# A graph network in f32: group sums in four PSUM banks, a pair's finishing a round later, and the counting as a loop

## The reference, cut to what matters

```
deg  = max(count of src, 1);  cnt = count of dst
msg  = (t1[src] + (x[src] * x[dst]) @ W2) / sqrt(deg[src] * deg[dst])      t1 = x @ W1
e    = leaky_relu(where(cnt > 0, t1 + segment_sum(msg, dst), 0) + b)
x1   = layernorm(x + e / max(norm(e), 1e-12))
agg  = segment_sum((x1 @ W.T + b1)[src], dst) / (count of dst + 1)
out  = layernorm(x1 + agg)
```

## Time and profile before

| | us |
|---|---|
| median of 3 runs (3993.7 to 3995.43) | 3994.8 |
| the profiled execution | 3996.79 |
| its span, first to last instruction | 3995.1 |

### The profile page before, as it was taken

The page is one execution under the profiler, slowest core; times in us unless marked ns, Lnnn a source line. Parts: engine busy times, 40 slices in busy tenths (PEclk is TensorE's granted clock), DMA queues, the critical chain, the costliest instruction groups (busy, mean ns, idle before and its releaser), DMA issues.

```text
span 3995.1 us, 42771 instructions
## 1 busy us (share of the span) xinstructions
PE 2991.8 (75%) x10186; PEld 1828.7 (46%) x10186; DVE 1864.8 (47%) x3536; ACT 664.3 (17%) x2054; POOL 2982.0 (75%) x3146
## 2 busy tenths in 40 slices
PE   4551777777777777777777877888888888878887
PEld 4441555555555555555433333344334343334443
DVE  9994555555555555555423333333333323232323
ACT  7992111111111111111100000000000000000000
POOL 7776777777777777777667777777777777777776
PEclk5555888988888888888867777666766666776667
DMA  8878455555555555555334443434443434343433
GB/s 256 272 233 309 150 156 155 155 156 155 156 155 155 156 158 156 158 155 156 116 94 118 117 118 116 119 115 120 115 120 115 120 115 120 115 121 114 120 115 107
DMA packets 294217, 582.43 MB, mean 146 GB/s; under 512 B 60723, under 2 KB 176100, under 8 KB 294180
## 3 DMA queue, kind: packets, MB, share of 16 engines
q0 software_dynamic: 150048, 409.93, 35.4%
q1 hardware_dynamic: 131364, 159.19, 11.9%
q10 hardware_dynamic: 12768, 12.85, 0.9%
HBM read 506.27 MB, written 75.45 MB: 146 GB/s over the span
## 4 chain that ended last, share of the span: by engine, by line
POOL 65%; issue 23%; POOLq 1%; PE 1%; DVE 0%; DVEq 0%; DMA 0%; ACT 0%; SPq 0%; ACTq 0%
POOL ring L478 65%; PE banks L1095 0%; POOLq L511 0%; DVEq L688 0%; POOLq L475 0%; PE banks L1121 0%; POOLq L476 0%; PE banks L1084 0%; DMA ring<-scaled_x,idx 0%; DMA ring<-x,idx 0%; POOL ring L488 0%; DMA x<-out_t 0%; DVE stats L917 0%; DVE out_t L929 0%; DVE big L850 0%
## 5 line engine op out<-in xcount | busy, mean ns | idle before, releaser
L1121 PE MATMUL banks<-ring,hot_space 128*128 128x257 f32 x6252 | 2470.7, 521 | 806.8 <-DMA ring<-x,idx 330.9
L1121 PEld LDWEIGHTS banks<-ring,hot_space 128*128 128x128 f32 x6252 | 1309.8, 242 | 1896.2 <-DMA ring<-x,idx 1058.0
L478 POOL DMA_INDIRECT ring<-x,idx x1563 | 1486.9, 951 | 505.3 <-issue 475.9
L478 POOL DMA_INDIRECT ring<-scaled_x,idx x1281 | 1221.2, 953 | 402.7 <-issue 402.7
L850 DVE SCALAR_TENSOR_TENSOR big<-banks,here_mask,big 128x257 f32 x784 | 343.9, 480 | 1604.5 <-PE banks L1121 1604.3
L806 DVE TENSOR_TENSOR hot_space<-banks,dst_rel 128x1024 f32<-128x1024 f32 x395 | 483.5, 1225 | 212.6 <-issue 210.8
L592 ACT COPY idx<-src_col 128x8 int32 (+1 forms) x392 | 77.3, 197 | 2145.7 <-PE banks L1121 2145.7
L488 POOL DMA_INDIRECT ring<-in_x,src_col x276 | 264.1, 957 | 84.1 <-issue 84.1
L554 ACT ACTIVATE dst_rel<-columns,halves 128x128 bf16<-128x128 f32 (+1 forms) x896 | 253.5, 374 | 23.8 <-PE banks L1042 19.6
L1035 PE MATMUL banks<-hot_space 128*128 128x98 bf16 x1120 | 104.2, 283 | 139.2 <-DVE hot_space L695 139.2
L1095 PE MATMUL banks<-w_s,a_t 128*128 128x256 f32 x784 | 179.3, 383 | 0.0
(11 more groups left out here) (115 smaller groups left out, 1193.2 us busy)
## 6 DMA issues: line engine op xcount, KB each, us to landing
kept_rows<-ring SPq DMA_DIRECT2D x94, 384.0 KB, 3.4
ring<-kept_rows SPq DMA_DIRECT2D x47, 768.0 KB, 5.5
ring<-x,idx POOLq DMA_INDIRECT x1563, 2.8
ring<-scaled_x,idx POOLq DMA_INDIRECT x1281, 2.8
dst_col<-in_src SPq DMA_DIRECT2D x47, 384.0 KB, 5.8
scaled_x<-big ACTq DMA_DIRECT2D x14, 896.0 KB, 17.5
x<-out_t SPq DMA_DIRECT2D x98, 128.0 KB, 2.4
x_t<-x SPq DMA_DIRECT2D x98, 128.0 KB, 2.3
```

The costliest lines, as they stand in the source:

```text
L478: g.indirect_dma_start(ring[:, u, 0:D], None, table[layer], bass.IndirectOffsetOnAxis(ap=idx[:, u:u + 1], axis=0)).then_inc(rows_in[u], 16)
L1121: last = nc.tensor.matmul(group_sum(k % SUMS), dst_hot[:, k % HOTS, u - k * GT, :], ring[:, u, 0:DW], start=u == tiles[0], stop=u == tiles ...
```

## The change

- `SUMS` is 4: group sums use banks 0 to 3, and VectorE's look-up of the kept factors (`found`) moves from banks 2 and 3 to banks 4 and 5, which the transposes use as well; TensorE therefore waits for `r_kept_made` before the transposes.
- A pair's transposes stand behind tile 24 instead of 20, its products behind the round's last tile. ScalarE's copies of the transposes stand in group 3.
- The finishing and moments of that pair stand in group 0 of the round after, its normalization in group 1, both ahead of the next pair's mix; ScalarE's roots stand behind quarter 0's indices there.
- The last round of a layer keeps the old places for its own pair and has the finishing of the pair before in addition.
- TensorE's counting is a loop over 35 passes (the first written out): two histogram batches with three step batches among them; the step batches that are left stand behind the loop.

```diff
-TURN_U = 20
-MIX_U = 24
+TURN_U = 24
+LAST_TURN_U = 20
+LAST_MIX_U = 24
-SUMS = 2
+SUMS = 4
-        found = banks[:, 2:4, 0:UNIT * NW].rearrange("p b (t n) -> p b t n", t=UNIT)
+        found = banks[:, 4:6, 0:UNIT * NW].rearrange("p b (t n) -> p b t n", t=UNIT)
...
+                    if sums and q == (LAST_K + 1 if last else GR - 1):
                         take_turned(layer, i - 1)
                     refill(layer, i, q)
-                    if finish and q == LAST_K + 1:
+                    if ended and q == 0:
+                        roots(layer, i - 2)
+                    if last and q == LAST_K + 1:
                         roots(layer, i - 1)
...
+                    if ended and k == 0:
+                        finish_sums(layer, i - 2, acc[:, bass.ds(2 * i - 4, 2), :])
+                        moments(layer, i - 2)
+                    if ended and k == LAST_K:
+                        norm(layer, i - 2)
+                    if sums and k == LAST_K and layer == 0:
+                        mix(i - 1, acc[:, bass.ds(2 * i - 2, 2), :])
+                    if last and k == LAST_K + 1:
+                        finish_sums(layer, i - 1, acc[:, bass.ds(2 * i - 2, 2), :])
+                        moments(layer, i - 1)
+                    if last and k == LAST_K + 2:
+                        norm(layer, i - 1)
...
-            for n in range(SRC_BATCHES):
-                hist_batch(n, n % 2, n == 0, False)
-                for k in range(n * STEP_BATCHES // SRC_BATCHES, (n + 1) * STEP_BATCHES // SRC_BATCHES):
-                    step_batch(k, k % 3, k == 0, k == STEP_BATCHES - 1)
+
+            def span(n, first):
+                for half in range(2):
+                    hist_batch(2 * n + half, half, first and half == 0, False)
+                    for third in ((0, 1), (2,))[half]:
+                        step_batch(3 * n + third, third, first and third == 0, False)
+
+            span(0, True)
+            with pe.Fori(1, SRC_BATCHES // 2) as n:
+                span(n, False)
+            for k in range(SRC_BATCHES // 2 * 3, STEP_BATCHES):
+                step_batch(k, k % 3, False, k == STEP_BATCHES - 1)
...
-                        if finish and u == TURN_U - 1:
+                        if finish and u == (LAST_TURN_U if last_one else TURN_U) - 1:
+                            if find:
+                                pe.wait_ge(r_kept_made, i + 1)
                             turn_halves(layer, i - 1)
-                        if finish and u == MIX_U - 1:
+                        if finish and u == (LAST_MIX_U if last_one else U) - 1:
                             products(layer, i - 1)
```

More of the change, by code:

```diff
@@ L633, in scale_kept, with round_ @@
                 last.then_inc(kept_scaled, 1)
-            def round_(layer, i, finish, with_kept=False):
+            def round_(layer, i, sums, ended, with_kept=False, last=False):
                 if with_kept:
@@ L638, in round_ @@
                 for q in range(4):
-                    if finish and q == LAST_K + 1:
+                    if sums and q == LAST_K + 1:
                         if layer == 0:
@@ L657, in _ @@
                         act.wait_ge(table1_whole, 1)
[L658 to L661, removed]
+                    round_(layer, 0, False, False)
+                    round_(layer, 1, True, False, layer == 0)
+                    with act.Fori(2, ROUNDS - 1) as i:
+                        round_(layer, i, True, True, layer == 0)
+                    round_(layer, ROUNDS - 1, True, True, last=True)
                     if layer == 0:
@@ L931, in norm, with round_ @@
                 ordered()
-            def round_(layer, i, finish, find=False):
+            def round_(layer, i, sums, ended, find=False, last=False):
                 block = load_block(i, 0)
@@ L967, in _ @@
                         v.wait_ge(acc_zeroed, ROUNDS)
[L968 to L972, removed]
+                    round_(layer, 0, False, False, layer == 0)
+                    round_(layer, 1, True, False, layer == 0)
+                    with v.Fori(2, KEPT_ROUNDS) as i:
+                        round_(layer, i, True, True, layer == 0)
+                    round_(layer, KEPT_ROUNDS, True, True)
+                    round_(layer, ROUNDS - 1, True, True, last=True)
                     if layer == 0:
@@ L1104, in find_places, with round_ @@
                 last.then_inc(places_found, 1)
-            def round_(layer, i, finish, end=U, with_kept=False, find=False):
+            def round_(layer, i, finish, end=U, with_kept=False, find=False, last_one=False):
                 for k in range(GR):
@@ L1144, in _ @@
                     round_(layer, KEPT_ROUNDS, True, with_kept=first)
-                    round_(layer, ROUNDS - 1, True, FINAL)
+                    round_(layer, ROUNDS - 1, True, FINAL, last_one=True)
                     turn_halves(layer, ROUNDS - 1)
```

## The result

Before, the median of 20 runs is 3995.11 us (3993.7 to 3997.84); after, of 20 runs, 4001.93 us (3999.51 to 4005.39). The ratio is 1.0016, 95% interval 1.0010 to 1.0022: 6.8 us slower, where the prediction had 5.5 us and "the same" by its bound of 0.2%. The profiled execution of after took 4001.94 us, its span is 4000.2 us; the prediction's sum for that execution was 4002.3 and 4000.6.

What follows compares the result with a forecast made beforehand. POOL's gathers (2844 at 1.25 us a step) were taken to bound the kernel. Late counts add 5.5 us, all other terms 0: span 3995.1 to 4000.6, median 3994.8 to 4000.3 us, 0.14% slower; range 3988 to 4008 us.

Steps and rivals of the forecast that it cites:

- The counting, 12.4 us late: Counting loop: seven step batches behind the last histogram batch make the counts whole at about 307.2 us instead of 294.8.
- How much reaches POOL, 5.5 us: Scaled table's store before layer 0: spare DMA bandwidth gives back part of the 12.4 us; 5.5 us remain, from 0 to 12.4.
- Rival 1: Table's store: none of the counts' lateness is given back, the whole 12.4 us reach POOL, 4007.2 us; chance 0.20.
- rival 3: Start of layer 0: early stores hold POOL until 371 anyway, the late table stays hidden, 3994.8 us; chance 0.12.
- rival 4: Counting loop: its jump starves the histogram, one us too much costing 34 us at the counts, about 4015 us; chance 0.03.
- Four banks, 0: Group sums in PSUM: four banks can remove only TensorE's 3.3 us of waits, off the chain; gain 0, from 0 to 3.3.
- Moved work has cover, 0: Pair work in the rounds: moved work stays within POOL's distance to the index copies, 21.3 us for quarter 0; costs nothing.
- the zeros of the prediction: Layers' border and the tail: they keep the old order, so they were costed at nothing.
- Strikes on gathers, 0: Gathers in both layers: VectorE's moved work lengthens as many gathers at other tiles; 0, between -20 and +20 us.
- rival 2: Gathers: the moved finishing no longer lengthens them, up to 20 us back, 3980.7 us, half of it 3990; chance 0.10.
- its mirror image: Gathers: the moved finishing lengthens them twice as much, 4020 us; chance 0.03.

Runs made afterwards that it cites:

- kernels 1 and 2: The kernel before with only the change's counting loop, 4003.3 us; the kernel before with the loop's batch order written out, no loop, 4002.17 us.
- Kernel 7: The kernel before with one step batch behind each histogram batch and 42 at the end, making the counts much later; one run, 4056.61 us.
- kernel 5: The kernel before with only four banks, the look-up in banks 4 and 5 and TensorE's wait for r_kept_made; 3996.54 us, ratio 1.0001.
- kernel 6: The kernel before with one useless VectorE maximum over 324 PSUM columns ahead of layer 1's finishing; 3990.25 us, ratio 0.9983.
- kernel 4: The change with the counting of before and layer 0 in the old order, so layer 1 alone has the new order; 3990.51 us, ratio 0.9984.
- kernels 3, 4 and 5: First of the three: the whole change with the counting of before, 3998.27 us, ratio 1.0003; the other two have their own lines.
- kernel 9: The whole change with the counting of before, plus the useless VectorE maximum twice in layer 0, ahead of finishing and mix; 3997.97 us, ratio 1.0006.

## Why the prediction was right, and where it was not

**The counting, 12.4 us late: right.** The counts came 12.8 us later (copied at 307.70 against 294.86), for the reason given: seven step batches of 2.25 us behind the last histogram batch, five of them without cover.

**How much reaches POOL, 5.5 us: right, a little small.** It was 6.1 us, and 5.3 and 5.9 in kernels 1 and 2; the kernels with the old counting start between 374.1 and 374.9, so a difference of half a microsecond means little here. Windows of after, beside the earlier trace rows:

```profile
290.00:304.00 14.00, 5.64 (x58) 4.35 (x56) 3.67 (x5) 13.03 (x48) 10.47 (x12) 0.50 0.64 200
304.00:317.00 13.00, 2.62 (x14) 1.79 (x14) 7.36 (x23) 11.06 (x30) 9.95 (x11) 0.50 0.66 218
317.00:378.00 61.00, 1.20 (x4) 0.58 (x4) 35.12 (x81) 12.10 (x19) 33.99 (x35) 0.50 1.03 372
```

While the table was late, the low rate was 200 to 218 GB/s; from the table's first store on it was 372 in the mean, near the 376 of the earlier trace rows. Kernel 7 shows the table alone at 341. If what is left at the end moves at that rate, the estimate becomes 12.4 x (376 - 212) / 341 = 6.0 us. Rival 1 (all of it at POOL, 386.5) and rival 3 (none of it, 374.2) fell by POOL's start at 380.3, rival 4 (the jump) by kernels 1 and 2. The Trainium skill (Runtime: NRT & Kernel Launch, Instruction fetch mechanics) has a taken branch stop the engine for a fetch when its target is outside the window; no such stop shows here: counts at 307.30 us with the loop, 307.76 without.

**Four banks, 0: right** (kernel 5), and the wait of TensorE for VectorE's additions is gone from the list of waits with no gain.

**Moved work has cover, 0: right.** Two of its figures were off. The prediction read a cover of 21.3 us for quarter 0 and more for the others; in fact quarter 1 has the shortest in layer 0, down to 17.0 us in before. And the prediction let it shrink by 3 to 4 us; it went to 15.4. Neither reached POOL. Border +0.1 and tail -0.7 us are the zeros of the prediction.

**Strikes on gathers, 0: right as a sum, wrong as argued.** The bound was right: against 0.945 us the gathers of before hold 20.4 us of lengthening (10.6 in layer 0, 9.8 in layer 1), those of after 20.3 (18.6 and 1.7). The step that failed is "the finishing follows a group's addition both before and after, with the same delay behind a gather, so I expect the same strikes at other tiles". The delay is not the same, and with it changes what is under way on VectorE when a gather starts. I sorted the lengthened gathers by the VectorE instruction that ends 0.82 us before the gather does. In layer 1 the pair of line 895 (line 900 in after) lengthened 45 gathers by 6.9 us together and now lengthens 2 by 0.3; the normalization went from 24 gathers and 2.1 us to 12 and 1.0. In layer 0 the finishing does the opposite: lines 883 and 886 (878 and 881 in before) lengthen 35 gathers by 4.4 us (before, 4 by 0.7), line 918 (913) 30 by 1.9 (before, 5 by 0.2), and the mix 45 by 7.3 (before, 34 by 5.7). Two such gathers in the timeline of after:

```profile
631.18 0.76 DVE L883 SCALAR_TENSOR_TENSOR e<-e 128x256 f32<-128x256 f32 x2
631.60 1.15 POOL L479 DMA_INDIRECT ring<-scaled_x,idx  x1 [0.30 <-issue]
...
1952.65 0.48 DVE L865 SCALAR_TENSOR_TENSOR halves<-x_t,root,big 128x256 f32<-128x256 f32 x1
...
1953.05 0.42 DVE L867 TENSOR_TENSOR halves<-x_t,big 128x256 f32<-128x256 f32 x1
1953.08 1.21 POOL L479 DMA_INDIRECT ring<-scaled_x,idx  x1 [0.30 <-issue]
1953.38 0.48 DVE L865 SCALAR_TENSOR_TENSOR halves<-x_t,root,big 128x256 f32<-128x256 f32 x1
1953.78 0.42 DVE L867 TENSOR_TENSOR halves<-x_t,big 128x256 f32<-128x256 f32 x1
```

The first gather ends at 632.75, 0.81 us after line 883's pair (631.94); the second at 1954.29, 0.82 us after the first instruction of line 867 (1953.47), with the mix's last two instructions under way in between.

That distance is the same in every trace. Counted over all eleven (before, after and the nine kernels): 783 gathers of the rounds started while a VectorE instruction with two tensor inputs from SBUF, begun at least 0.10 us earlier, had 0.15 us or more still to run. All 783 were lengthened, and each ended 0.81 to 0.83 us after that instruction. With a tensor_scalar there, which has one tensor input from SBUF, 416 of 434 were. With any other instruction there, one with an input from PSUM or a bn_stats, 45 of 6238 were; with the pair of line 900 (one input from PSUM) none of 160. In layer 1 kernel 6 confirms this by moving the pair; in layer 0 it rests on the count alone.

So rival 2 was right in layer 1 and its mirror image in layer 0, each by 8 us. That they cancel is chance: kernel 4 keeps one without the other and is 6.8 us faster than before. Two terms of 8 us, each of either sign, put the outcomes around the forecast at some 3984, 4000 and 4016 us; my range held only the middle one, and that the time fell into it is partly luck.

The Trainium skill (SBUF — State Buffer, Who interferes with whom) says that a VectorE instruction with at most one SBUF input, outside the two-port modes, does not contend with GpSimd. Line 900 agrees: its tensor inputs are a PSUM bank and one tile in SBUF, beside a scalar per partition, and it lengthened none of 160. Line 895, the mix, line 883 and the square sums (two SBUF inputs) agree with the page's other rule. Whether the tensor_scalars ran in a two-port mode is not shown by any trace.

## What to carry to other kernels

When a loop replaces an evenly spread order, look at what is left behind the last pass: there the slower producer has lost its cover, and only spare bandwidth between it and the consumer gives some of it back. When one engine's step sets the time and other engines lengthen it, a term of "same work, other place" is not zero but a throw of the dice for each loop; look at which instruction of the other engine is under way when a step starts, measure the loops one by one, and keep the order of each loop that came out well. A useless half microsecond on an idle engine can be worth more than a saved one, but the moment that it finds holds for that code alone.

## What the runs showed of the hardware

- A gather of 128 rows takes 0.945 us and its pause 0.30 in every kernel. Of the 31284 gathers of the rounds in the eleven traces 1444 took over 0.965 us, up to 1.33 in layer 0 (kernels 3, 4 and 5). 1399 of these ended 0.81 to 0.83 us after a VectorE instruction with two tensor inputs from SBUF, or a tensor_scalar on SBUF, that had begun before the gather; the other 45 are not explained.
- An added reduction of 0.50 us a round made the kernel 6.5 us faster (kernel 6 against its before).
- A table in pieces of 896 KB on ScalarE's queue alone was written at 341 GB/s (kernel 7); from the table's first store to its landing, with the early gathers and their stores beside it for most of that time, the DMA engines moved 376 (before) and 372 (after).
- In kernel 9 the means of a layer whose code was not changed moved by 3 ns. So where VectorE's instructions fall against POOL's steps was not set by that layer's code alone, and a gain by strikes is not a property of one function.
